# Batch 1's normalised rows are turned by VectorE out of an HBM round trip, with their low parts on GpSimd, and the router's logits move behind the first key products

## What is computed

```python
xn = layernorm(x)                                   # x: (2, 1024, 512)
q, k, v = split(xn @ w_qkv.T + b_qkv)
s  = softmax(q @ k.T / sqrt(512)) @ v @ w_out.T + b_out
logits = xn @ router_w + router_b                   # (2, 1024, 8), top 2 of 8
moe = sum over the two experts of w_e * silu(xn @ expert_w[e] + expert_b[e])
y  = xn + moe @ proj_w + proj_b
g  = silu(norm_w * y / sqrt(mean(y*y) + 1e-6))
x  = x + s * g
```

## Time and profile before

| | |
|---|---|
| median of three runs | 486.54 us (485.69 to 486.70) |
| the profiled execution | 485.28 us, of which the span of the profile is 483.5 us |
| TensorE busy | 472.6 us, 98% of the span |
| TensorE weight loads | 391.4 us, 81% |
| VectorE busy | 323.2 us, 67% |
| ScalarE busy | 213.3 us, 44% |
| GpSimd busy | 222.3 us, 46% |
| DMA | 115.77 MB, 239 GB/s over the span |

### The profile page before, as it was taken

How to read it: one execution, slowest core, us unless ns; L and a number is a source line. 1 busy time by engine, 2 the same in 40 slices (tenths; PEclk the granted TensorE clock), 3 DMA queues, 4 the chain that set the end, 5 groups by cost and what they waited for, 6 DMA issues and landing times.

```text
span 483.5 us, 7144 instructions
## 1 busy us (share of the span) xinstructions
PE 472.6 (98%) x2148; PEld 391.4 (81%) x2149; DVE 323.2 (67%) x479; ACT 213.3 (44%) x309; POOL 222.3 (46%) x323
## 2 busy tenths in 40 slices
PE   9899799999999999999999999999999999999995
PEld 7778677888888888888888888888888888888884
DVE  3975772777651536888888888762597755857752
ACT  3683563143331163744544444323655441644550
POOL 5687310006887849600300000755567873367234
PEclk9999899999999999999999999999999999999999
DMA  8966999947979599979699655987555864435512
GB/s 309 335 215 245 381 355 401 368 146 249 309 259 343 177 334 316 251 220 281 205 270 275 199 193 180 319 287 284 164 165 158 271 183 166 155 133 171 174 45 85
DMA packets 78190, 115.77 MB, mean 239 GB/s; under 512 B 6656, under 2 KB 36368, under 8 KB 78160
## 3 DMA queue, kind: packets, MB, share of 16 engines
q1 hardware_dynamic: 65072, 79.72, 51.3%
q0 software_dynamic: 6896, 23.36, 13.7%
q10 hardware_dynamic: 6192, 12.32, 7.2%
HBM read 66.09 MB, written 49.28 MB: 239 GB/s over the span
## 4 chain that ended last, share of the span: by engine, by line
PE 92%; DMA 2%; DVE 2%; issue 1%; ACTq 1%; SPq 1%; ACT 1%
PE ab L1698 22%; PE ab L1699 22%; PE ab L1700 22%; PE sc L1698 7%; PE sc L1699 7%; PE sc L1700 7%; PE tp L1704 2%; DMA xb<-in_x 2%; PE tp L1733 2%; ACTq L954 1%; PE sc L1762 1%; PE sc L1765 1%; DVE stats L1240 1%; SPq L525 0%; DVE xt_l L1251 0%
## 5 line engine op out<-in xcount | busy, mean ns | idle before, releaser
L836 POOL DMA_INDIRECT y<-y_scratch,pos x32 | 33.4, 1042 | 78.0 <-DMA y_scratch<-yt_so 63.6
L1698 PE MATMUL ab<-W,st_h 128*128 x156 | 60.7, 389 | 0.0
L1699 PE MATMUL ab<-W,st_h 128*128 x156 | 60.7, 389 | 0.0
L1700 PE MATMUL ab<-W,st_l 128*128 x156 | 60.7, 389 | 0.0
L819 POOL DMA_INDIRECT rows_scratch<-xb,pos x32 | 31.4, 982 | 51.8 <-DVEq L1376 43.6
L1698 PE MATMUL sc<-xt_h,t_h 128*128 128x512 f32 x128 | 50.1, 391 | 0.0
L1700 PE MATMUL sc<-xt_h,t_l 128*128 128x512 f32 x128 | 49.9, 390 | 0.0
L1699 PE MATMUL sc<-xt_l,t_h 128*128 128x512 f32 x128 | 49.8, 389 | 0.0
L1094 ACT CAST st_h<-tp 128x512 fp32r<-128x512 f32 x39 | 22.9, 587 | 43.1 <-PE ab L1700 42.2
L1459 DVE TENSOR_REDUCE small<-sc 128x1 f32<-128x1024 f32 x16 | 19.5, 1222 | 26.5 <-PE sc L1700 20.4
L1698 PEld LDWEIGHTS ab<-W,st_h 128*128 128x128 f32 x156 | 29.3, 188 | 6.1
(11 more groups left out here) (290 smaller groups left out, 1235.1 us busy)
## 6 DMA issues: line engine op xcount, KB each, us to landing
rows_scratch<-xn ACTq DMA_DIRECT2D x3, 3328.0 KB, 20.1
xb<-in_expert_w POOLq DMA_DIRECT2D x6, 1024.0 KB, 9.2
xn<-rows_scratch SPq DMA_DIRECT2D x48, 128.0 KB, 3.1
xg<-rows_scratch SPq DMA_DIRECT2D x44, 128.0 KB
y_scratch<-yt_own SPq DMA_DIRECT2D x20, 256.0 KB, 3.0
y_scratch<-yt_so SPq DMA_DIRECT2D x19, 256.0 KB, 2.8
p_scratch<-prob SPq DMA_DIRECT2D x9, 512.0 KB
rows_scratch<-xs SPq DMA_DIRECT2D x16, 256.0 KB, 6.7
```

Of the source, the lines that this page charges most:

```text
L836: pool.indirect_dma_start(y[:, q, :], None, y_d, bass.IndirectOffsetOnAxis(pos[:, GB * s + p:GB * s + p + 1], 0))\
L1698: nc.tensor.matmul(dst, lh, rh, start=start, stop=False)
L1699: nc.tensor.matmul(dst, lh, rl, start=False, stop=False)
L1700: return nc.tensor.matmul(dst, ll, rh, start=False, stop=stop)
```

## The change

**Batch 1 leaves TensorE.** ScalarE normalises batch 1's tiles in place, in `xb1`. SP stores each to HBM as before and then, for each pair of tiles, issues four DMAs (`spread_pair`) that bring the rows back into `xb` in blocks. VectorE's block transpose (`turn_spread`) writes the turned tile into one of the four `xs` buffers in SBUF, ScalarE's `hi` copies the high part from there, and GpSimd, no longer VectorE, makes the low part. Tiles 12 to 15 get a home of their own (`wk_h`, `wk_l`, free after the last fold). TensorE's eight `turn` of batch 1, four transposes each, are gone.

**Order.** On TensorE the four folds stand one behind the other with the two `sum_rows` between them; `sum_rows(0)` puts its small product into `tp`. Batch 0's logits follow, then the first key product, batch 1's first logits, two key products, batch 1's last logits, the fourth key product and `turn_logits`. On VectorE `fold_query_bias` moves ahead of the folds' low parts, two `turn_spread` stand before the last fold's low part, two more before `fold_key_bias`, and the other four between the low parts of the key products. On ScalarE all normalisations come early, and `hi(8)` and `hi(9)` stand before the last fold's high part.

**Zeros and scatter.** ScalarE issues one of the three zero fills, behind value tile 4; SP issues the other two, behind the last `spread_pair`. The eight early loads of rows to be sent are gone: GpSimd scatters batch 1's tiles first, from where they lie in `xb1`, and batch 0's after them, loaded as slots come free. GpSimd starts the expert loads when the last tile is turned.

```diff
@@ -401,6 +401,24 @@
+def turned_whole(g):
+
+    return tp[:, g % 2, :, :] if g < GB else xs[:, g % 4, :].rearrange("p (c n) -> p c n", c=KC)
+
+def turned_rows(g):
+
+    w = slice(g % QB * P, (g % QB + 1) * P)
+    if g < GB:
+        return xt_h[:, :, g * P:(g + 1) * P], xt_l[:, :, g * P:(g + 1) * P]
+    if g < GB + QB:
+        return bt_h[:, :, w], bt_l[:, :, w]
+    return wk_h[:, :, w], wk_l[:, :, w]
+
+def clear_slots(eng, n):
+
+    w = slice(n * SLOT_TILES // 3, (n + 1) * SLOT_TILES // 3)
+    eng.dma_start(rows_t[:, w, :], zeros.to_broadcast([P, w.stop - w.start, D])).then_inc(zero_in, 16)
+
@@ -538,21 +556,40 @@
         sp.wait_ge(xn_ready, g + 1)
-        sp.dma_start(rows_g[home(g)], xs[:, g % 4, :]).then_inc(xn_st[g % 4], 16)
+        sp.dma_start(rows_g[home(g)], xs[:, g % 4, :] if g < GB else xb1[:, g - GB, :])\
+            .then_inc(xn_st[g % 4], 16)
+
+    def spread_pair(n):
+
+        g = GB + 2 * n
+        for k in (g, g + 1):
+            sp.wait_ge(xn_st[k % 4], 16 * (k // 4 + 1))
+        for a in range(4):
+            sp.dma_start(xb[32 * a:32 * (a + 1), 2 * n:2 * n + 2, :].rearrange("p t (r f) -> p (t r) f", r=4),
+                         rows_q[home(g):home(g) + 2, a, :, :, :].rearrange("t s r f -> s (t r) f"))\
+                .then_inc(x_in[n], 16)
     load_half(0)
-    for g in range(G):
+    for g in range(GB):
         if g == 4:
...
         store_row(g)
+    for g in range(GB, GB + 4):
+        store_row(g)
+    for n in range(KC):
+        spread_pair(n)
+        if n < 2:
+            store_row(GB + 4 + 2 * n)
+            store_row(GB + 5 + 2 * n)
+    for n in (1, 2):
+        clear_slots(sp, n)
     sp.wait_ge(fold_l, 2 * KC)
...
     def load_to_send(g):
-        if g >= GB:
-            sp.wait_ge(sent[g % GB], 32)
-        sp.dma_start(sent_rows[:, g % GB, :], rows_g[home(g)]).then_inc(send_in[g % GB], 16)
+        sp.wait_ge(sent[g], 32)
+        sp.dma_start(sent_rows[:, g, :], rows_g[home(g)]).then_inc(send_in[g], 16)
@@ -568,8 +605,6 @@
         sp.wait_ge(xn_st[q], 4 * G)
-    for g in range(GB):
-        load_to_send(g)
     def load_bias(e):
@@ -596,14 +631,14 @@
     store_s(0)
-    for g in range(GB, GB + 4):
+    for g in range(4):
         load_to_send(g)
     store_s(1)
-    load_to_send(GB + 4)
-    load_to_send(GB + 5)
+    load_to_send(4)
+    load_to_send(5)
     store_s(2)
-    load_to_send(GB + 6)
-    load_to_send(GB + 7)
+    load_to_send(6)
+    load_to_send(7)
     store_s(3)
@@ -797,7 +832,12 @@
-    pool.wait_ge(xn_ready, G)
+    for g in range(GB, G):
+        high, low = turned_rows(g)
+        pool.wait_ge(hi_done, g + 1)
+        pool.tensor_tensor(low, turned_whole(g), high, ALU.subtract).then_inc(lo_done, 1)
+
+    pool.wait_ge(t_done, G)
     for e in BY_BUFFER[0:2]:
@@ -813,15 +853,17 @@
     pool.wait_ge(routed, 1)
-    for g in range(G):
-        pool.wait_ge(send_in[g % GB], 16 * (g // GB + 1))
+    for n in range(G):
+        g = (n + GB) % G
+        if n >= GB:
+            pool.wait_ge(send_in[g], 16)
         for pos in (pos1, pos2):
...
                                     sent_rows[:, g % GB, :], None).then_inc(sent[g % GB], 16)
-        if g < 2 * KC:
-            early_low(g // KC, g % KC)
-        elif g >= 3 * KC:
-            early_low(2, g % KC)
+        if n < 2 * KC:
+            early_low(n // KC, n % KC)
+        elif n >= 3 * KC:
+            early_low(2, n % KC)
     for c in range(KC):
@@ -923,10 +965,11 @@
     def normalise(g):
-        if g >= 4:
+        if 4 <= g < GB:
             act.wait_ge(t_done, g - 3)
             act.wait_ge(xn_st[g % 4], 16 * (g // 4))
-        nc.scalar.activation(xs[:, g % 4, :], xbs[g // GB][:, g % GB, :], ACT.Identity, bias=shift[:, g:g + 1],
+        whole = xbs[g // GB][:, g % GB, :]
+        nc.scalar.activation(xs[:, g % 4, :] if g < GB else whole, whole, ACT.Identity, bias=shift[:, g:g + 1],
                              scale=rstd[:, g:g + 1]).then_inc(xn_ready, 1)
@@ -936,8 +979,10 @@
         act.wait_ge(t_done, g + 1)
-        high = xt_h[:, :, g * P:(g + 1) * P] if g < GB else bt_h[:, :, g % QB * P:(g % QB + 1) * P]
-        nc.scalar.copy(high, tp[:, g % 2, :, :]).then_inc(hi_done, 1)
+        if g >= GB + QB:
+            act.wait_ge(fold, 2 * KC)
+        high = turned_rows(g)[0]
+        nc.scalar.copy(high, turned_whole(g)).then_inc(hi_done, 1)
@@ -947,11 +992,6 @@
-
-    def clear_slots(n):
-
-        w = slice(n * SLOT_TILES // 3, (n + 1) * SLOT_TILES // 3)
-        act.dma_start(rows_t[:, w, :], zeros.to_broadcast([P, w.stop - w.start, D])).then_inc(zero_in, 16)
@@ -982,32 +1022,33 @@
         v_hi(0, t)
-        if t >= GB - 3:
+        if t == GB - 4:
             act.wait_ge(zero_set, 1)
-            clear_slots(t - GB + 3)
+            clear_slots(act, 0)
     act.wait_ge(ln_done, 3)
...
     fold_high(KC)
+    for g in range(GB + 4, G):
+        normalise(g)
+    fold_high(KC + 1)
+    fold_high(KC + 2)
     act.wait_ge(qk_split, 6)
...
     hi(GB + 1)
-    fold_high(KC + 1)
-    normalise(GB + 4)
-    normalise(GB + 5)
+    fold_high(KC + 3)
     hi(GB + 2)
     hi(GB + 3)
-    fold_high(KC + 2)
-    normalise(GB + 6)
-    normalise(GB + 7)
-    fold_high(KC + 3)
     act.wait_ge(rt_done, 1)
-    for g in range(GB + QB, G):
-        hi(g)
-    act.wait_ge(rt_done, 2)
     nc.scalar.copy(lt[0], sc[0:2 * NP, 0, :, :].rearrange("p a n -> p (a n)")).then_inc(lt_out, 1)
     t_hi(0, 0, 0)
-    act.wait_ge(rt_done, 3)
+    hi(GB + 4)
+    hi(GB + 5)
+    t_hi(0, 0, 1)
+    hi(GB + 6)
+    hi(GB + 7)
+    t_hi(0, 0, 2)
+    act.wait_ge(rt_done, 2)
     nc.scalar.copy(lt[1], sc[0:2 * NP, 1, :, :].rearrange("p a n -> p (a n)")).then_inc(lt_out, 1)
@@ -1053,8 +1094,7 @@
-    for n in range(1, KC):
-        t_hi(0, 0, n)
+    t_hi(0, 0, 3)
     exp_0(0)
@@ -1244,11 +1284,20 @@
     def lo(g):
-        w = slice(g % QB * P, (g % QB + 1) * P)
-        high, low = ((xt_h[:, :, g * P:(g + 1) * P], xt_l[:, :, g * P:(g + 1) * P]) if g < GB else
-                     (bt_h[:, :, w], bt_l[:, :, w]))
+        high, low = turned_rows(g)
         dve.wait_ge(hi_done, g + 1)
-        vec.tensor_tensor(low, tp[:, g % 2, :, :], high, ALU.subtract).then_inc(lo_done, 1)
+        vec.tensor_tensor(low, turned_whole(g), high, ALU.subtract).then_inc(lo_done, 1)
+
+    def turn_spread(g):
+
+        k = g - GB
+        dve.wait_ge(x_in[k // 2], 64 + 16 * (2 if k < 4 else 1))
+        if g < GB + 4:
+            dve.wait_ge(t_done, GB)
+        else:
+            dve.wait_ge(lo_done, g - 3)
+        vec.transpose(turned_whole(g).rearrange("p c (r s) -> p c r s", r=4),
+                      xb[:, k, :].rearrange("p (r q c) -> p c r q", r=4, c=KC)).then_inc(t_done, 1)
@@ -1295,7 +1344,7 @@
         dve.wait_ge(vecs, 2)
-        link(vec.tensor_reduce(rb_bc[:, E:E + 1], ab[:, 1, 0:KC], AX.X, ALU.add))
+        link(vec.tensor_reduce(rb_bc[:, E:E + 1], tp[:, 0, 0, 0:KC], AX.X, ALU.add))
         pick(0, rw[:, :, E]).then_inc(pre_done, 1)
@@ -1430,18 +1479,17 @@
     weigh_rows(1)
+    fold_query_bias()
     fold_low(KC)
-    lo(GB)
-    lo(GB + 1)
     fold_low(KC + 1)
-    fold_query_bias()
-    lo(GB + 2)
-    lo(GB + 3)
     fold_low(KC + 2)
+    turn_spread(GB)
+    turn_spread(GB + 1)
+    fold_low(KC + 3)
+    turn_spread(GB + 2)
+    turn_spread(GB + 3)
     fold_key_bias()
-    fold_low(KC + 3)
-    for g in range(GB + QB, G):
-        lo(g)
+    turn_spread(GB + 4)
@@ -1486,10 +1534,14 @@
     routing = choose()
-    for n in range(KC):
-        t_lo(0, 0, n)
-        if n == 2:
-            read_logits()
+    t_lo(0, 0, 0)
+    turn_spread(GB + 5)
+    turn_spread(GB + 6)
+    t_lo(0, 0, 1)
+    turn_spread(GB + 7)
+    t_lo(0, 0, 2)
+    read_logits()
+    t_lo(0, 0, 3)
     next(routing)
@@ -1719,9 +1771,7 @@
             pe.wait_ge(ab_read, 2 + GB)
-            nc.tensor.matmul(ab[:, 1, 0:KC], ones[:, :], prod, start=True, stop=True)
-        else:
-            pe.wait_ge(pre_done, 2)
+            nc.tensor.matmul(tp[:, 0, 0, 0:KC], ones[:, :], prod, start=True, stop=True)
         nc.tensor.matmul(ab[:, m, :], ones_r[:, :], sums[m][:, 0, :], start=True, stop=False)
@@ -1754,7 +1804,7 @@
     def logit_rows(b, m):
-        high, low = (xt_h, xt_l) if b == 0 else (bt_h, bt_l)
+        high, low = (xt_h, xt_l) if b == 0 else (bt_h, bt_l) if m == 0 else (wk_h, wk_l)
         keys = slice(m * 512, (m + 1) * 512) if b == 0 else slice(0, 512)
@@ -1819,36 +1869,27 @@
     fold_keys(FOLDS[0])
-    turn(GB)
-    turn(GB + 1)
     fold_keys(FOLDS[1])
     sum_rows(0)
-    turn(GB + 2)
-    turn(GB + 3)
     fold_keys(FOLDS[2])
...
     pe.wait_ge(pre_done, 3)
-    pe.wait_ge(lo_done, GB + QB)
-    pe.wait_ge(fold_l, KC + 1 + FOLDS.index(2))
-    logit_rows(1, 0).then_inc(rt_done, 1)
-    turn(GB + QB)
-    turn(GB + QB + 1)
     pe.wait_ge(fold_l, KC + 1 + FOLDS.index(0))
     logit_rows(0, 0)
-    turn(GB + QB + 2)
-    turn(GB + QB + 3)
     pe.wait_ge(fold_l, KC + 1 + FOLDS.index(1))
...
```

(8 more changed lines are left out.)

## The result

| | before | changed |
|---|---|---|
| median of 11 runs each, side by side | 485.69 us (484.62 to 486.71) | 488.46 us (487.13 to 489.77) |
| ratio | 1 | 1.0055, 95% interval 1.0044 to 1.0066 |
| span of the profile | 483.5 us | 487.3 us |
| TensorE, VectorE, ScalarE, GpSimd busy | 472.6, 323.2, 213.3, 222.3 us | 470.0, 325.4, 213.3, 232.3 us |
| bytes moved | 115.77 MB | 115.77 MB |

What follows compares the result with a forecast made beforehand. TensorE, busy 98% of the span, bounds it. Removing transposes, pause and slow clock wins some 8.7 us; waits of 1.0, 4.2, 1.9 and slow clock 1.7 take it back: 486.54 - 0.1, about 486.4 us, range 483.2 to 489.0.

Steps and rivals of the forecast that it cites:

- rival (3): Batch 1's row stores land in about 7 us instead of 2, delaying the first key product: 489.4 us, chance 0.14.
- rival (4): The third wait, before batch 1's last logits, costs clock too, 1.7 us more: 488.1 us, chance 0.09.
- The wait for GpSimd's sums: New TensorE wait before sum_rows(0), for GpSimd's rounded sums: about 1 us.
- The first key product's wait: New TensorE wait for VectorE's key bias, start at 68.15 instead of 63.96: 4.2 us.
- The low part of tile 15: Third new TensorE wait, before batch 1's last logits, for GpSimd's low part: 1.9 us.
- The clock fell: Low clock after the first key product's wait, lasting 3.4 us almost wholly in work: 1.7 us lost, bounds 0 and 1.9.
- rival (2): VectorE's SBUF transpose turn_spread takes 0.70 instead of 1.06 us: 484.6 us, chance 0.10.
- (1): TensorE's clock holds through the 4.2 us wait, 1.7 us less: 484.7 us, chance 0.14.
- (5): TensorE's new waits are hidden, VectorE or ScalarE reaching pre_done 4 some other way: 7.8 us less, 478.6 us, chance 0.05.
- (a): Zero fills moved, one on ScalarE and two late on SP: slack about 20 us before tile 1's exponent, costing nothing.
- (c): Expert loads start when tile 15 is turned, near 80 instead of 66 us: costs nothing.
- the removed pause of 3.49 us: TensorE's idle time up to 52.90 us, put down to ScalarE held 4.69 us issuing the third zero fill.

Runs made afterwards that it cites:

- the key product first: Changed kernel with fold_key_bias ahead of turning tiles 8 to 11 and ScalarE's last fold_high ahead of hi(8) and hi(9): 487.42 us, ratio 1.0050.
- TensorE's order: The one with the mw store late as well, plus key product 1 before batch 1's first logits, tile 15's turn and hi(14) earlier: 482.90 us, ratio 0.9938.
- the one with the mw store late as well: Changed kernel with the key product first and SP's mw store behind the fourth load of probabilities: 483.35 us, ratio 0.9958.
- the control: Kernel before with only its mw store moved behind the fourth load of probabilities: 485.42 us, ratio 0.9995.
- the nw store behind: Kernel of TensorE's order with the nw store behind the first load of probabilities and ScalarE's first early copy behind exp_0(2): 480.00 us, ratio 0.9881.

## Why the prediction was wrong

**What held.** The rebuilt stretch held nearly throughout. (That the 488.46 us lie inside the stated range is luck: its upper end stands on rivals (3) and (4), and neither came.) The wait for GpSimd's sums came with 1.1 us (forecast 1.0). The first key product started 21.5 us behind the first fold (68.45 - 46.93), where the forecast had 68.15 against the first fold's start in the kernel before, 21.7:

```profile
46.43 0.40 PE L1698 MATMUL sc<-pt_h,t_h 128*128 128x512 f32 x1
```

The first key product's wait was 3.89 (4.2). The low part of tile 15 was waited for 1.85 (1.9). The clock fell:

```profile
68.00:72.00 4.00, 3.55 (x11) 2.82 (x12) 1.45 (x2) 0.61 (x1) 1.32 (x2) 0.70 1.05 410
72.00:76.00 4.00, 4.00 (x17) 2.34 (x16) 2.30 (x3) 1.70 (x3) 1.30 (x1) 0.88 1.04 403
```

Shortfalls of 0.30 and 0.12 of 4 us are 1.7 us; at 0.5 of full clock that is 3.4 us at 1.2 GHz in the first key product, as forecast. `turn_spread` took 2.07 for two and 1.10 for one, so rival (2) falls: the Trainium skill's sentence on strides (SBUF — State Buffer, Door 1: The DMA port swizzle) doesn't carry over to this transpose even with both ends in SBUF. The first of them started straight behind VectorE's low parts at 60.30, waiting for no DMA, so rival (3) falls; before the last fold's low part VectorE waited 1.68 us for ScalarE, as foretold:

```profile
60.30 2.07 DVE L1299 STREAM_TRANSPOSE xs<-xb 128x512 f32<-128x512 f32 x2
```

Rivals (1) and (5) fall with the clock and the waits above, and rival (4) since the clock is at 1.00 from 80 to 90 us, behind the third wait.

**What failed is the paragraph on "the other edits"**, steps (a) and (c), each costed at nothing, where 2.8 us were lost. (a) asked of the two fills who waits for the zeros (the exponent of tile 1, near 101), found 20 us of slack there, and stopped. It named `nw` and `mw` behind the fills on SP's queue but not what stands behind these: the probabilities' store at 97 us, a transfer of half a megabyte whose landing TensorE's work hangs on through VectorE. (c) asked who waits for the expert weights and not whom their 2 MB delay when they are moved from 66 to 82 us. The rows for the sum were there: fills landing in 10.6 to 36.6 us and a DMA share of 1.02 and 1.05 at 385 and 377 GB/s say that these engines have a queue and not slack. What was missing is the balance of bytes. The zeros asked for some 20 us later are 6.8 MB, in front of 4.2 MB of stores and 2.1 MB of weights. These 13.1 MB at the 407 GB/s of 90 to 100 us are 32 us from 64.12, so 96.3 at the earliest, by an estimate that leaves out the round trips' remains; the store was asked for at 97.42, and the engines were full until about 101. That balance would have shown that the store comes into the backlog. It would not have given the 2.8 us.

**The sentence behind it failed too**: "Behind 87.92 TensorE pauses nowhere before the tail; what is won or lost up to there reaches the end whole". No pause is not the same as slack. In the kernel before, VectorE had waited 0.75 us for this load, and its low part was finished at 108.34, 1.96 us before TensorE took it up at 110.30. VectorE's 2.65 us went beyond that at the first pause and, by way of the scatters, at the third. And a gain ahead of 88 us is not passed on while the engines are full: the key product first passed on 1.0 of 2.8 us, TensorE's order 0.5 of 3.5, until the stores were out of the way.

**A step right in its number and wrong in its reason** is the removed pause of 3.49 us. It was put down to the issue of the third fill alone. In the kernel before with its fills moved, a wait for GpSimd's sums took its place, 3.83 us. In the changed kernel the transposes that stood there are gone, and the pause with them, whatever the fill does; this is a reading of the two lists. The sum came out since it rebuilt the list and didn't lean on the cause.

**What stays open.** The expert loads move as well, and how much of the 2.8 us belongs to the fills and how much to the expert loads alone was not separated: holding 1 MB of weights shortened the store by 1.9 us and cost more elsewhere. That late fills are enough for a backlog was shown in the kernel before, not by giving the changed kernel its old fills back.

## What to carry to other kernels

When a large transfer moves on a queue, don't ask only who waits for it: add up the bytes outstanding at each small transfer that an engine does wait for, over all queues, and compare with the rate at which the engines are seen to work when full. A stretch in which the DMA share falls below 1 ahead of a stretch where it is 1 is lost capacity, and it can come back as a late transfer further on. And where such a late transfer ends the path, a better order on the compute engines passes on little until it is mended: here the same reordering was worth 1.0 us before and 2.2 us after.

## What was not expected of the hardware

**Issuing a transfer can hold a queue's engine for long.** The issue of one 2 MB store takes 0.38 us where no fills stand ahead of it on SP's own queue (68.80 in the kernel before, with the 16 engines full, 1.03 in 60 to 70 us) and 8.49, even 14.82 us where two do. The Trainium skill, DMA: Bandwidth & Descriptors, section "Issuing engines are not separate DMA queues", calls the time that it takes to initiate a transfer usually small relative to the transfer; by an estimate at 407 GB/s those 2 MB are some 5 us, so here the issue took longer than moving the bytes would have; from issue to landing the store took 26.7 us. On ScalarE, which also computes, the same effect held an engine for 4.69 us.

**The clock's fall is not settled by TensorE's list.** The key-first kernel and the one with the mw store late as well have the same list on TensorE up to here and nearly the same pause (2.10 and 2.06 us, ending at 68.53 and 68.59). In the first the clock fell:

```profile
68.00:70.00 2.00, 1.47 (x4) 0.56 (x5) 1.88 (x3) 0.67 (x3) 1.77 (x2) 0.63 1.05 410
70.00:72.00 2.00, 2.00 (x6) 0.82 (x5) 0.89 (x1) 0.55 (x1) 1.28 (x1) 0.51 1.05 409
```

and in the second it stayed at 2.4 GHz:

```profile
68.00:70.00 2.00, 1.41 (x7) 0.57 (x8) 1.79 (x3) 0.69 (x3) 1.78 (x2) 1.00 1.05 409
70.00:72.00 2.00, 2.00 (x10) 1.56 (x9) 0.95 (x1) 0.61 (x1) 1.36 (x2) 1.00 1.05 410
```

The scores started at 85.23 and 83.72, 1.5 us apart. The mean clock differs between executions of one kernel too: beside the control and the nw store behind, those of the kernel before with a mean clock of 0.996 had spans of 483.0 to 484.0 us, those at 0.990 spans of 483.8 to 484.9; in which stretch they differ isn't recorded. A pause of 2 us is thus neither safe nor surely paid for, and a difference of 1.5 us between two profiles can be this alone.
